# Issue order of the Q and K loads, and the residual bias per tile, in an eight-item audio tower on one core

## What is computed

```python
h = layernorm(x.reshape(8, 1500, 80) @ W.T + b) * g + be
h = gelu(h)
n = layernorm(h)                              # no gain, no shift
q, k, v = n @ Wq.T + bq, n @ Wk.T + bk, n @ Wv.T + bv   # 16 heads of 16
a = softmax(q @ k.T / 4) @ v                  # per head, 1500 keys
h = h + (a @ Wo.T + bo)                       # bo: the bias of this change
out = h + layernorm(layernorm(h)) * ln_g + ln_b
```

## Time and profile before

| what | value |
|---|---|
| median of 3 runs | 2430.32 us (2424.12 to 2434.16) |
| the profiled execution's own time | 2416.48 us |
| its span, first to last instruction | 2414.7 us |
| mean granted TensorE clock | 0.972 |
| busy: ACT / PE / DVE / POOL | 2145.6 / 2093.9 / 967.1 / 369.4 us |
| busy share of the span: ACT / PE / DVE / POOL | 89% / 87% / 40% / 15% |
| moved by DMA | 138.46 MB, 57 GB/s mean |

### The profile page before, as it was taken

The page is one execution under the profiler, slowest core; times in us unless marked ns, Lnnn a source line. Parts: engine busy times, 40 slices in busy tenths (PEclk is TensorE's granted clock), DMA queues, the critical chain, the costliest instruction groups (busy, mean ns, idle before and its releaser), DMA issues.

```text
span 2414.7 us, 123554 instructions
## 1 busy us (share of the span) xinstructions
PE 2093.9 (87%) x57132; PEld 921.6 (38%) x57132; DVE 967.1 (40%) x2171; ACT 2145.6 (89%) x2332; POOL 369.4 (15%) x495
## 2 busy tenths in 40 slices
PE   4668999889997999979999899988999799988885
PEld 1322444334443444434443344434444344432223
DVE  6433334543255333543345433553335533332114
ACT  0069999989998999989999899999999899999993
POOL 2210101220022110211012110221102210110003
PEclk8889999999999999999999999999999999999998
DMA  2222222221222322122321223123211122212101
GB/s 57 78 52 57 63 68 61 47 78 46 68 51 52 78 68 57 33 56 70 78 62 42 59 61 78 43 60 76 68 48 41 45 75 73 66 44 52 35 9 35
DMA packets 110255, 138.46 MB, mean 57 GB/s; under 512 B 32299, under 2 KB 89706, under 8 KB 109730
## 3 DMA queue, kind: packets, MB, share of 16 engines
q1 hardware_dynamic: 107194, 128.64, 21.2%
q10 hardware_dynamic: 2536, 1.83, 0.3%
HBM read 55.16 MB, written 61.44 MB: 48 GB/s over the span
## 4 chain that ended last, share of the span: by engine, by line
PE 49%; ACT 30%; DVE 8%; issue 8%; DVEq 2%; POOL 2%; DMA 1%; SPq 0%; POOLq 0%; ACTq 0%
ACT prob L503 29%; PE PS L928 21%; PE PS L898 13%; PE PS L846 8%; DVE HL L584 2%; DVE HL L582 2%; PE PS L858 2%; PE PS L873 2%; PE PS L832 1%; DVE On L644 1%; PE PS L823 1%; DVEq L652 1%; DVE z L564 0%; DVE Hs L540 0%; POOL rs L384 0%
## 5 line engine op out<-in xcount | busy, mean ns | idle before, releaser
L503 ACT ACTIVATE prob<-PS 125x1000 f32<-125x1000 f32 x2304 | 2102.3, 1057 | 200.9 <-PE PS L898 194.0
L928 PE MATMUL PS<-prob,Vst 64*32 64x500 f32 (+1 forms) x18432 | 1214.8, 585 | 8.3 <-issue 5.2
L898 PE MATMUL PS<-QA,KA 64*32 64x500 f16 (+1 forms) x18432 | 963.5, 379 | 150.9 <-ACT prob L503 136.4
L898 PEld LDWEIGHTS PS<-QA,KA 64*32 64x32 f16 (+1 forms) x18432 | 285.6, 90 | 1041.7 <-ACT prob L503 970.5
L928 PEld LDWEIGHTS PS<-prob,Vst 64*32 64x32 f32 (+1 forms) x18432 | 366.9, 106 | 46.1 <-issue 15.4
L846 PE MATMUL PS<-zT,w_qk 64*32 64x250 f32 x6144 | 246.3, 381 | 21.5 <-DVE HL L584 15.2
L582 DVE TENSOR_SCALAR HL<-PS,b_qk 128x500 f16<-128x500 f32 x96 | 70.9, 739 | 362.5 <-PE PS L846 341.1
L397 POOL TENSOR_TENSOR sq<-HL 128x2000 bf16<-128x2000 f16 x24 | 84.5, 3520 | 718.1 <-DVE HL L584 718.1
L858 PE MATMUL PS<-w_v,zT 64*32 64x128 f32 (+1 forms) x6144 | 136.7, 271 | 42.7 <-DVE HL L584 18.3
L630 DVE COPY Osb<-PS 128x500 f32<-128x500 f32 x96 | 65.1, 678 | 245.5 <-PE PS L928 245.3
L404 POOL TENSOR_TENSOR Y<-Hs,be_ln 125x256 f32<-125x256 f32 x96 | 70.3, 732 | 550.7 <-DVE Hs L651 543.4
(11 more groups left out here) (78 smaller groups left out, 887.3 us busy)
## 6 DMA issues: line engine op xcount, KB each, us to landing
qk_halves_scratch<-HL SPq DMA_DIRECT2D x384, 125.0 KB
QA<-qk_halves_scratch SPq DMA_DIRECT2D x64, 375.0 KB
KA<-qk_halves_scratch SPq DMA_DIRECT2D x64, 375.0 KB
oT<-On SPq DMA_DIRECT2D x384, 31.2 KB
out<-Y SPq DMA_DIRECT2D x24, 500.0 KB
X<-in_x SPq DMA_DIRECT2D x16, 234.4 KB
thin<-Osb SPq DMA_DIRECT2D x96, 7.8 KB
Den<-thin SPq DMA_DIRECT2D x96, 7.8 KB
```

Of the source, the lines that this page charges most:

```text
L503: act.activation(prob[0:T, 2 * (w % 6):2 * (w % 6) + 2, :], PS[0:T, 2 * (w % 2):2 * (w % 2) + 2, 0:QC], ACT.Exp, scale=scl)\
L898: last = pe.matmul(PS[lo:hi, bank, 0:QC], KA[rows, G % 2, h // 2, t * T + lo:t * T + hi], QA[rows, G % 2, h // 2, c * QC:(c + 1) * QC], st ...
L928: last = pe.matmul(PS[lo:lo + 2 * HD, bank + r, 0:QC], Vst[rows, b % 2, t, g * HG + j, :], prob[rows, (HG * t + j) % 12, :], start=(t == 0 ...
```

## The change

The four transfers of `load_group` become four calls with a `part`; the waits stay with part 0. In units 1, 4 and 7 they stand at `k` = 13, 16, 19, 22, in unit 10 at `k` = 14, 17, 20, 23. Parts 0 and 1 are the transfers of `QA`, 2 and 3 those of `KA`. `add_bias` becomes four instructions of 125x256, with the signal on the last.

```diff
-            def load_group(G):
+            def load_group(G, part):
                 b, g = G // NG, G % NG
-                if G >= 1:
-                    sp.wait_ge(s_ld, at(s_ld, 64 * G))
-                if G >= 2:
-                    sp.wait_ge(s_sc, at(s_sc, WIN * NC * (G - 1)))
-                if g == 0:
-                    sp.wait_ge(s_st, at(s_st, 16 * 16 * NC * (b + 1)))
-                for w, dst in ((0, QA), (1, KA)):
-                    for par in range(2):
-                        src = qk_s[b, w, 4 * g + par:4 * g + 4:2, :, :]
-                        sp.dma_start(dst[64 * par:64 * par + 64, G % 2, :, :], src.rearrange("i r q -> r i q"))\
-                          .then_inc(s_ld, 16)
+                w, par = part // 2, part % 2
+                if part == 0:
+                    if G >= 1:
+                        sp.wait_ge(s_ld, at(s_ld, 64 * G))
+                    if G >= 2:
+                        sp.wait_ge(s_sc, at(s_sc, WIN * NC * (G - 1)))
+                    if g == 0:
+                        sp.wait_ge(s_st, at(s_st, 16 * 16 * NC * (b + 1)))
+                dst, src = (KA if w else QA), qk_s[b, w, 4 * g + par:4 * g + 4:2, :, :]
+                sp.dma_start(dst[64 * par:64 * par + 64, G % 2, :, :], src.rearrange("i r q -> r i q")).then_inc(s_ld, 16)
...
-                            if u % NC == 1 and u < NU - 2:
-                                load_group(n // NC + 1)
-                        if u == NU - 2 and k == 16 and b + 1 < B:
-                            load_group(n // NC + 1)
+                        if u % NC == 1 and u < NU - 2 and k in (13, 16, 19, 22):
+                            load_group(n // NC + 1, (k - 13) // 3)
+                        if u == NU - 2 and k in (14, 17, 20, 23) and b + 1 < B:
+                            load_group(n // NC + 1, (k - 14) // 3)
...
             def add_bias(b, k):
-                h = Hs[:, hslot(b, k * CT):hslot(b, k * CT) + CT, :]
                 pool.wait_ge(s_z, at(s_z, b * NC + k + 1))
                 if b == 0 and k == 0:
                     pool.wait_ge(s_wo, 16 * 5)
-                pool.tensor_tensor(h, h, b_o[:, :].unsqueeze(1).broadcast_to([T, CT, D]), ALU.add).then_inc(s_hb, 1)
+                for e in range(k * CT, k * CT + CT):
+                    h = Hs[:, hslot(b, e), :]
+                    ins = pool.tensor_tensor(h, h, b_o[:, :], ALU.add)
+                ins.then_inc(s_hb, 1)
```

More of the change, by code:

```diff
@@ L302, in run @@
                     store_halves(0, i)
-                load_group(0)
+                for part in range(4):
+                    load_group(0, part)
                 for n in range(B * NU):
```

## The result

The changed kernel takes **2416.64 us** (median of 6 runs, 2408.52 to 2420.64) against 2427.65 us for the kernel before in the same measurement (2424.12 to 2440.2). The ratio is **0.9937, 95% interval 0.9909 to 0.9965**: 0.63% faster, about 15 us, with an interval of 8 to 22 us. (The two medians alone are 11.0 us apart; the ratio is not the quotient of the medians.) The forecast was 4 us and "within 0.5%"; the measured time lies in the range, the size of the gain was wrong by a factor of more than three.

A forecast was written before the change was run, and what follows sets the result against it. ACT's exponentials, fed by PE's scores, were taken to bound the kernel, so PE's stalls cost time. Loads −8 and bias +4 gave −4 us: 2430.3 to 2426 us, range 2413 to 2440.

The forecast's parts named there:

- What the change does on SP: Units 4 and 7 of items 0 to 6: 14 groups become Q loads, four stores, K loads; units 1 and 10 unchanged.
- The cause of the issue stalls: PE stands 16.9 us before value projections with no semaphore missing; its instruction fetch was said to stand behind the loads.
- the rival in which nothing is won: Stalls in units 5 and 8 only move or have another cause: 0 from loads, +4 from bias, 2434 us; chance 0.22.
- the price of the stalls: Stalls in units 5 and 8: splitting the loads was to save 8 us, between 0 and 10.1.
- four fifths: Share of the 10.1 us taken as won, −8 us, since the second load pair meets PE's stock partly used up.
- bound of 10.1: ACT's loss from eleven stalls, 5.8 us in unit 5 and 4.3 in unit 8, taken as the full possible gain.
- The bias: Four POOL pieces at (2, 18) of items 1 to 6 cost 6 × 0.7 = +4 us, between −4 and +7.
- a later start of the last output's chain: End of unit 2: L404 starts 0.1 to 1.1 us later, taken as +0.7, passed through DVE to PE's turn.
- The forecast growth of PE's wait to "about 18 us": PE's wait for DVE's sums (L632) before unit 3's first turn grows from 14.1 to about 18 us.
- All of the gain: Stalls go wholly and POOL's chain ends no later: −10.1 and 0 to −4, so −12 to −14, 2417 us; chance 0.22.
- Sums late: Unit 8: K's loads ahead of `thin` delay DVE's sums 1.95 us in seven items, 13.7 us; 2448 us; chance 0.11.

The follow-up runs named there:

- loads_only: The changed kernel with the old one-instruction add_bias, loads still split; 2413.0 us, ratio 0.9943 to the kernel before.
- three_one: The changed kernel with the old one-instruction add_bias and three loads ahead of the four stores, one behind; 2412.1 us, ratio 0.9937 to the kernel before.
- stores_first: The kernel before with the four loads of units 4 and 7 (items 0 to 6) issued together behind the four stores; 2461.4 us, ratio 1.0156.
- unit2_loads: Against the kernel before: loads paced by SP waits, unit 1's moved into unit 2, next item's first one-instruction bias behind DVE's sums; 2372.1 us, ratio 0.9775.

## Why the prediction was wrong in size and right in kind

*What the change does on SP.* Right: 14 groups reordered, units 1 and 10 untouched, the named periods without effect where SP waits for nothing.

*The cause of the issue stalls.* Right. The fetch of PE's instructions comes late behind an unbroken train of loads; loads_only, three_one, stores_first and unit2_loads show it from four sides, and the packet records show the fetch. The rule on queue rows of the Trainium skill (*DMA: Bandwidth & Descriptors*, "Queues, rings and completion order") led to the rival in which nothing is won. The measurement decides against that rival: at the 11 stalls the fetch, on its own queue, started 0.5 to 2.5 us before the end of the loads, 6.5 to 8.8 us after the one before it.

*The step that failed: the price of the stalls.* The forecast put −8 us, four fifths of a bound of 10.1, the idle time of ACT just ahead of the late scores. Measured are −0.57%, 13.8 us of 2426, and 14.4 us in the lengths of units 5 and 8. Two errors, both on the same side. First, the bound was no bound, since it counted only ACT's idle time before the late exponential. The exponentials' records are 1.06 us long but follow each other every 0.88 us. In item 5 of the kernel before the late one of unit 8 comes 2.12 us after its forerunner with 1.06 us of idle time, 1.24 over the normal step, and the next one takes 1.05 us; so that unit took 23.6 us instead of 22.2, 1.4 for a gap of 1.06. Eleven times 0.36 on top of the 10.1 are the measured 14. In the kernel before, the items without a stall in unit 8 (3, 4, 6) already had 22.2, against 23.3 to 24.0 in the others: that would have given 5.6 us for unit 8, where 4.3 were put. Second, the cut to four fifths: the second pair of loads left no stall, so all of it was won.

*The bias.* The price of the pieces was put at +4 us through a later start of the last output's chain, 0.7 us each time. It was 0.06 in item 3 and at most that in the others. Four pieces and one L669 between them took 2.98 us, where 3.15 were taken for the pieces alone and up to 0.98 more for the two that break in; and L404 had waited 0.69 us before, which swallowed the rest. The pieces do not add up from their own 0.73 us: in the 18 groups where DVE does not break in, each starts 0.68 to 0.70 us after the last and four take 2.8 us, and L669 adds 0.2 and not its own 0.49. The measured cost is +1.7 us (−1.7 to +5.1). The forecast growth of PE's wait to "about 18 us" came true (18.8), by luck, for another reason than the one given: PE came sooner, the work it waits for did not come later.

*The rivals.* "All of the gain" (−12 to −14 us) came nearest, with a chance of 0.22. Its loads part is what happened, though its bias part (a chain that gets shorter) did not; and its terms, −10.1 and 0 to −4, add up to −10 to −14. "Sums late" did not occur: the wait for `thin` before the reciprocal is 69.1 us in total against 67.9.

## What to carry to other kernels

When an engine with a long unrolled program stalls in the middle of a group of instructions with no semaphore to wait for, look at what fills the DMA engines 5 to 10 us earlier; look for late starts of the packets that carry its instructions, break the train of large transfers, and try another place for it, since the place changed its price here. Transfers spread over loop steps in the code are only spread on the chip if the issuing queue waits for something at each step. Price a stall by the whole length of the stage with and without it, not by its own idle time; and judge a wait from a common start, since it also grows when the waiting engine comes sooner.

## What the runs showed that was not expected

The same train of four loads cost PE 0.4 to 1.6 us in one place (and nothing in three of 14) and 1.7 to 3.0 in another four periods later, where the whole kernel took 33 us more. Taking one POOL instruction of 2.4 us out of a chain, six times, gave 18 us; behind the shorter wait the clock did not drop: unit 3 fell from 26.8 to 23.1 us each time, 3.7 us for 1.5 us of PE's wait. And the two steps that the change only brushed, the loads of unit 1 and the place of the bias, were worth more than the change itself: the kernel with both runs in 2372 us, 2.25% under the kernel before (interval 2.06% to 2.44%).
